# Attention and mixture layers on one core: no second score product in two of four head groups, an upper bound of the scores in its place, other slots in the last stage, first roots off GpSimd

## The reference

```python
q = _l2norm(q) * q_scale
k = _l2norm(k) * k_scale
sim = jnp.einsum('bhid,bhjd->bhij', q, k) * ATTN_SCALE
dist = -jnp.abs(cols[None, :] - (rows[:, None] + NUM_NULL_KV)).astype(sim.dtype)
sim = sim + dist[None, None] * slopes[None, :, None, None]
sim = jnp.where(causal_mask[None, None], neg, sim)
attn = jax.nn.softmax(sim, axis=-1)
out = jnp.einsum('bhij,bhjd->bhid', attn, v)
```

## Time and profile before

| | |
|---|---|
| three runs | 1751.26, 1755.71, 1756.75 us, median 1755.71 |
| the profiled execution | 1750.87 us, span 1749.1 us |
| mean granted clock of TensorE | 0.946 of 2.4 GHz |
| PE busy | 1565.2 us, 89% of the span |
| DVE, ACT, POOL busy | 1036.5, 774.6, 596.5 us |
| DMA | 73.77 MB, mean 42 GB/s |

### The profile page before, as it was taken

How to read it: one execution, slowest core, us unless ns; L and a number is a source line. 1 busy time by engine, 2 the same in 40 slices (tenths; PEclk the granted TensorE clock), 3 DMA queues, 4 the chain that set the end, 5 groups by cost and what they waited for, 6 DMA issues and landing times. The chain is left out here.

```text
span 1749.1 us, 28227 instructions
## 1 busy us (share of the span) xinstructions
PE 1565.2 (89%) x8941; PEld 740.7 (42%) x8941; DVE 1036.5 (59%) x2399; ACT 774.6 (44%) x1364; POOL 596.5 (34%) x597
## 2 busy tenths in 40 slices
PE   5799999999999999999999999999399549888898
PEld 2344444444444444444444444444267334333332
DVE  4455646666565655657656566665523277777775
ACT  3345454454544445544454444544144234444432
POOL 4253452534436354353543515442300331111000
PEclk8799999999999999999999999999599759999999
DMA  3502030320202202021120200000411100000000
GB/s 109 170 7 76 23 99 1 111 70 1 70 4 73 61 28 70 1 70 37 41 76 1 70 8 6 10 3 6 158 48 55 38 13 7 13 13 13 7 7 13
DMA packets 106718, 73.77 MB, mean 42 GB/s; under 512 B 5250, under 2 KB 100762, under 8 KB 106319
## 3 DMA queue, kind: packets, MB, share of 16 engines
q1 hardware_dynamic: 104526, 67.76, 12.7%
q0 software_dynamic: 2048, 4.20, 0.8%
HBM read 24.23 MB, written 47.71 MB: 41 GB/s over the span
## 5 line engine op out<-in xcount | busy, mean ns | idle before, releaser
L826 ACT ACTIVATE P<-S,keyb 128x386 f32<-128x386 f32 (+7 forms) x512 | 296.6, 630 | 375.8 <-PE S L609 375.6
L605 PE MATMUL S<-QT,KT 64*128 64x512 f32 (+5 forms) x1792 | 378.5, 478 | 8.3 <-DVE KT L964 6.3
L1200 POOL TENSOR_TENSOR rn<-nm,half 128x12 f32<-128x12 f32 x128 | 299.5, 2344 | 94.4 <-DVE nm L901 94.4
L1223 POOL TENSOR_SCALAR_AFFINE_SELECT P<-P 128x256 f32<-128x256 f32 (+1 forms) x256 | 156.3, 611 | 478.9 <-ACT P L826 478.7
L1004 DVE TENSOR_TENSOR Psum<-Psum,P 128x1796 f32<-128x1796 f32 (+7 forms) x256 | 281.9, 1101 | 37.5 <-PE O L630 18.3
L630 PE MATMUL O<-P,V 128*64 128x512 f32 (+5 forms) x1536 | 255.4, 436 | 4.0 <-POOL P L1223 3.3
L605 PEld LDWEIGHTS S<-QT,KT 64*128 64x128 f32 (+1 forms) x1792 | 158.4, 179 | 193.2 <-issue 183.6
L609 PE MATMUL S<-GQ,GK 64*128 64x512 bf16 (+5 forms) x896 | 150.9, 303 | 0.0
L466 PE MATMUL W<-xT,wts 128*128 128x512 f32 x256 | 141.3, 646 | 9.8 <-DVE QT L960 7.2
L1071 DVE TENSOR_TENSOR part<-W,rden 128x512 f32<-128x512 f32 x128 | 82.4, 686 | 83.4 <-PE W L678 83.4
L630 PEld LDWEIGHTS O<-P,V 128*64 128x64 f32 (+1 forms) x1536 | 80.0, 135 | 108.6 <-issue 94.2
(11 more groups left out here) (244 smaller groups left out, 2118.6 us busy)
## 6 DMA issues: line engine op xcount, KB each, us to landing
xg<-zero SPq DMA_DIRECT2D x16, 1216.0 KB, 10.6
yg<-zero SPq DMA_DIRECT2D x16, 1216.0 KB, 9.6
wts<-in_w_qkv SPq DMA_DIRECT2D x16, 384.0 KB, 3.8
gu<-in_gu SPq DMA_DIRECT2D x1, 2816.0 KB, 10.4
xb<-xg SPq DMA_DIRECT2D x40, 64.0 KB, 1.8
yg<-yb SPq DMA_DIRECT2D x40, 64.0 KB, 1.6
X<-in_x SPq DMA_DIRECT2D x4, 512.0 KB, 4.5
wo<-in_w_out SPq DMA_DIRECT2D x16, 128.0 KB, 2.3
```

What stands on the lines that cost most here:

```text
L605: nc.tensor.matmul(S[hh][0:m, at + c:at + c + w], KT[d, r, p, jt * P:jt * P + m], QT[d, r, p, Q0[jt] + c:Q0[jt] + c + w], start=True, stop ...
L826: nc.scalar.activation(probs(p, jt)[0:m, hh, 0:n], S[hh][0:m, at:at + n], ACT.Exp, bias=keyb[0:m, r, (2 * p + hh) * NKT + jt:(2 * p + hh) ...
L1200: nc.gpsimd.tensor_tensor(rn[:, c, u], nm[:, c, u], powers, ALU.pow).then_inc(rn_ok, 1)
L1223: nc.gpsimd.affine_select(own, own, [[0, 2], [1, w]], ALU.is_ge, 0.0, base=NNULL if jt == 0 else 0, channel_multiplier=-1).then_inc(cut, 1)
```

## The change

`FLAT` is the groups whose largest slope times 512 is below 40: groups 2 and 3, so the turns with n % 4 of 2 or 3, eight of 16 (the flat turns).

- In a flat turn `scores` issues no second product, and the first one ends the accumulation and signals ScalarE. Turns that prepare a flat one leave out both edge jobs: PE's transposes, ScalarE's copy to GQ, DVE's steps for E and `ee`, and 4 of the 12 root columns on GpSimd.
- In its place the keys' table of these groups is lifted by 40 and lowered by the largest score possible: the largest |q_scale x k_scale x 8|, found before attention by a matmul of ones with a diagonal (`lim`), a maximum over it, and one subtraction in `tabs`.
- The first turn's roots are made by ScalarE (square root) and DVE (a reciprocal and a Newton step, seven small operations a half) instead of GpSimd, `parts` stand in steps 5 and 10 instead of 9 and 12, the tables of laps are shorter, and ScalarE loads its tables at chosen places.
- In the last stage both choices, the weights and the weighings change slots; the share goes behind the down product; turned normed rows and router go one slot earlier; ScalarE takes the sigmoids' exponential ahead of the distances'. GpSimd gathers chunk 1 behind the first root instead of ahead of it.

```diff
+FLAT = tuple(g for g in range(NG) if slopes()[HG * g] * SEQ / 2 < LIFT)
...
+    for g in FLAT:
+        key[:, g * HG:g * HG + HG] += LIFT
...
-                return [k for k in AT if k[0] != "X" or n - 1 in HALF_AT]
+                return [k for k in AT if (k[0] != "X" or n - 1 in HALF_AT) and not (k in EDGE and flat_turn(n))]
...
-            AT_LAPS = {6: (2, 3), 9: (4, 5), 13: (6, 7)}
-            DVE_LAPS = {4: (2, 3), 9: (4, 5), 13: (6, 7)}
-            ACT_LAPS = {7: (2, 3), 10: (4, 5), 14: (6, 7)}
+            AT_LAPS = {6: (2, 3), 8: (4, 5), 9: (6, 7)}
+            DVE_LAPS = {4: (2, 3), 6: (4, 5), 8: (6, 7)}
+            ACT_LAPS = {7: (2, 3), 8: (4, 5), 10: (6, 7)}
...
-                            nc.tensor.matmul(S[hh][0:m, at + c:at + c + w], KT[d, r, p, jt * P:jt * P + m],
-                                             QT[d, r, p, Q0[jt] + c:Q0[jt] + c + w], start=True, stop=False)
-                        for hh in range(2):
+                            last = nc.tensor.matmul(S[hh][0:m, at + c:at + c + w], KT[d, r, p, jt * P:jt * P + m],
+                                                    QT[d, r, p, Q0[jt] + c:Q0[jt] + c + w], start=True, stop=flat_turn(t))
+                            if flat_turn(t) and c + w == n:
+                                last.then_inc(qk, 1)
+                        for hh in range(0 if flat_turn(t) else 2):
...
+                        pe.wait_ge(lim_ok, 3)
+                        nc.tensor.matmul(S[1][:, 512:512 + P], rows_n[:, 0:P], rows_n[:, P:2 * P], start=True, stop=True)
...
+                    nc.scalar.activation(flat[:, 0], nm[:, c].rearrange("p u n -> p (u n)"), ACT.Sqrt).then_inc(flat_ok, 1)
...
+                act.wait_ge(consts, 1)
+                nc.scalar.activation(warmed[:], half[:, 1, 0:1], ACT.Sqrt).then_inc(warm, 1)
...
+                act.wait_ge(warm, 1)
+                nc.scalar.activation(warmed[:], half[:, 1, 0:1], ACT.Exp).then_inc(warm, 1)
...
+                    nc.vector.tensor_scalar(b_, flat[:, 0], 1e-15, None, ALU.max).then_inc(step_ok, 1)
+                    nc.vector.reciprocal(y, b_).then_inc(step_ok, 1)
+                    nc.vector.tensor_tensor(a_, y, v, ALU.mult).then_inc(step_ok, 1)
+                    nc.vector.tensor_tensor(b_, a_, y, ALU.mult).then_inc(step_ok, 1)
+                    nc.vector.tensor_scalar(a_, b_, -0.5, 1.5, ALU.mult, ALU.add).then_inc(step_ok, 1)
+                    nc.vector.tensor_tensor(out, y, a_, ALU.mult).then_inc(step_ok, 1)
+                    nc.vector.tensor_tensor(rn[:, c, :, 2 * HG:], rn[:, c, :, 2 * HG:], nm[:, c, :, 2 * HG:],
+                                            ALU.mult).then_inc(step_ok, 1)
...
+                nc.vector.tensor_reduce(lim[:, 2:3], S[1][:, 512:512 + P], AX.X, ALU.max).then_inc(lim_ok, 1)
                 nc.vector.tensor_copy(w1q[:, 1, :], S[1][:, 0:D]).then_inc(m_ok, 1)
+                nc.vector.tensor_scalar(keys, keys, lim[:, 2:3], None, ALU.subtract).then_inc(lim_ok, 1)
...
-                    nc.gpsimd.tensor_tensor(rn[:, c, u], nm[:, c, u], powers, ALU.pow).then_inc(rn_ok, 1)
+                    w = (2 if flat_turn(n) else 3) * HG
+                    nc.gpsimd.tensor_tensor(rn[:, c, u, 0:w], nm[:, c, u, 0:w], powers[:, 0:w], ALU.pow).then_inc(rn_ok, 1)
...
-                    elif live(u - 2):
-                        share(u - 2, j)
                     if 0 <= k - LAG < KS:
                         down(k - LAG)
                     if j == 0 and live(u):
                         rows_turned(u)
-                    if j == 0 and live(u - 2):
-                        share(u - 2, 0)
+                    if live(u - 2):
+                        share(u - 2, j)
...
+                    if j == 3 and live(u - 1):
+                        logits(u - 1)
+                    if j == 3 and live(u + 1):
+                        arrive(u + 1)
                     if j == 4 and live(u - 1):
-                        logits(u - 1)
+                        pick_one(u - 1)
+                        pick_other(u - 1)
+                    if j == 5 and live(u - 1):
+                        weights(u - 1)
                     if j == 5 and live(u):
                         shares(u)
-                        weigh(u, 0)
-                    if j == 6 and live(u - 1):
-                        pick_one(u - 1)
-                    if j == 7 and live(u - 1):
-                        pick_other(u - 1)
+                    if j in (6, 7) and live(u):
+                        weigh(u, j - 6)
...
-                get_chunk(1)
                 periods(slot)
```

More of the change, by code:

```diff
@@ L241, in build @@
             scl = sb("scl", [P, 3], F32, sc)
+            lim = sb("lim", [P, 3], F32, sc)
             sums = sb("sums", [P, 2, 32], F32, sc)
@@ L277, in build @@
             xtr = sb("xtr", [P, CH], F32, sc)
+            flat = xtr[:, 0:4 * 4 * 3 * HG].rearrange("p (a n) -> p a n", a=4)
+            warmed = xtr[:, CH - 1:CH]
             rtop = sb("rtop", [P, 2, NB], F32, sc)
@@ L329, in build, with flat_turn, edged @@
             PREP_BEFORE = (("T1", "E0", ("R0", None), ("S00", "S01")), ("P00", "P02", ("P03", None), ("N0", None)))
+            def flat_turn(n):
+                return n % NG in FLAT
+            def edged(n, c):
+                return sum(0 if flat_turn(m) else 14 for m in range(n)) + (0 if flat_turn(n) else 7 * c + 7)
             def jobs(n):
-                return [k for k in AT if k[0] != "X" or n - 1 in HALF_AT]
+                return [k for k in AT if (k[0] != "X" or n - 1 in HALF_AT) and not (k in EDGE and flat_turn(n))]
             def prepared(n, k):
@@ L578, in prepare @@
                     for c in range(2):
-                        if AT[EDGE[c]] == at:
+                        if AT[EDGE[c]] == at and not flat_turn(n):
                             edges(n, c, alone)
@@ L804, in prepare @@
                                 square(n, c, j)
-                        if AT[EDGE[c]][:-1] == str(s):
+                        if AT[EDGE[c]][:-1] == str(s) and not flat_turn(n):
                             edges_out(n, r, c)
@@ L870, in _ @@
                             nc.scalar.copy(nkT[hh * DH:(hh + 1) * DH], src[hh * DH:(hh + 1) * DH, :, hh, :]).then_inc(null_te, 1)
+                    for c in range(2):
+                        if AT[TURNED[c]][:-1] == str(s):
+                            first_roots(c)
                     for h in ACT_LAPS.get(s, ()):
                         settled(h)
+                act.wait_ge(warm, 1)
+                nc.scalar.activation(warmed[:], half[:, 1, 0:1], ACT.Exp).then_inc(warm, 1)
                 turn(0, 0, True)
@@ L931, in parts @@
                         nc.vector.tensor_tensor(rres[:, k], own if k == 0 else rres[:, 0], R[:, at:at + 4, :, k], ALU.subtract).then_inc(r_ok, 1)
-                        dve.wait_ge(e_ok, ek + 2 * k + 2)
-                        hold(dve)
-                        nc.vector.tensor_copy(E[:, at:at + 4, :, :, k], heads(ee[:, k + 1])).then_inc(e_ok, 1)
+                        if edge:
+                            dve.wait_ge(e_ok, ek + 2 * k + 2)
+                            hold(dve)
+                            nc.vector.tensor_copy(E[:, at:at + 4, :, :, k], heads(ee[:, k + 1])).then_inc(e_ok, 1)
                         dve.wait_ge(r_ok, rk + 2 * k + 2)
@@ L1800, in slot @@
                         gate_up(u - 2, j)
[L1801 to L1807 removed]
+                    if j == 0 and live(u - 1):
+                        form(u - 1)
+                    if j == 0 and live(u - 2):
+                        combine(u - 2)
                     if 0 <= k - LAG < KS:
@@ L1817, in slot @@
                         last_turned(u - 3)
+                    if j == 2 and live(u - 1):
+                        normed_turned(u - 1)
                     if j == 3 and live(u - 1):
-                        normed_turned(u - 1)
-                    if j == 4 and live(u - 1):
                         route(u - 1)
@@ L2093, in slot @@
                         distances(u)
-                    if j == 4 and live(u + 1):
-                        arrive(u + 1)
-                    if j == 6 and live(u):
-                        weigh(u, 1)
-                    if j == 8 and live(u - 1):
-                        weights(u - 1)
                     if live(u - 2):
@@ L2139, in slot @@
                         norm1.pool_shift(pool, n4(u - 3))
-                    if j == 4 and live(u + 1):
+                    if j == 3 and live(u + 1):
                         norm.pool_shift(pool, n2(u + 1))
+                        if u < 0:
+                            get_chunk(1)
                         if live(u + 3):
```

90 lines of the change are left out of this document (63 added, 27 removed).

## The result

| kernel | median of 4 runs, us | range, us | ratio to before, 95% interval |
|---|---|---|---|
| before | 1753.49 | 1750.06 to 1756.75 | |
| changed | 1726.74 | 1724.99 to 1729.34 | 0.9849 [0.9823, 0.9875] |

The account below looks back on a forecast made before the run. PE was taken to bound attention (1127 of 1177 us busy). From the profiled 1750.9: attention -49, before it -3, six periods +1, filling +5.5 gave 1705.4, forecast 1708 with half the median's distance added; range 1687 to 1722.

Parts of the forecast that it names:

- The price of the second product: Attention, flat turns: start to start, 2.8 us a pair of heads, 5.6 a turn; 39 for seven turns, 3.5 for the last.
- What is late next: Attention, turn ends: PE's waits for roots and scales grow a little; 0.3 us a turn, 2 us in all, given back.
- The clock at the heads: Attention turn heads: clock fell behind 0.92 and 0.52 us waits at a quarter of heads; used for the last stage.
- a rival of many falls within flat turns: Attention: without the dense bf16 product the clock falls within flat turns; eight falls in each give 1808 us; chance 0.02.
- The edge transposes: Attention, eight preparations of flat turns: 16 groups of eight transposes at 0.55 us, 8.8 us saved on PE.
- Before attention: Ahead of the first score: roots on ScalarE and DVE instead of GpSimd give -3 us, between -7 and +2.
- the filling: Start of the last stage: choosing and weights now precede the weighings, so transposes come later; +5.5 us, between +2 and +8.
- The ring of the last stage: One period: transposes of sums, gate, silu, DVE's stretch to the second weighing and back; 38.3 us at full clock.
- The clock on it: Last stage: a fall in each period, 2.7 to 2.9 us, making periods 41.0 to 41.2; six periods +1.
- The chance of 0.20 for no falls: Rival: the clock stays up in the last stage, six periods at 38.3 save 16 us, 1692 with the addition; chance 0.20.
- attention gives back half: Rival: in flat turns GpSimd's cuts or the exponentials arrive after PE; +22 us, 1730 as a run; chance 0.10.

Follow-up runs that it names:

- the held runs: Second product, or edge transposes, put back into the changed kernel with later DVE additions and idle products (1707.79 us): 1735.60 and 1716.47 us.
- held_all: Changed kernel with later DVE additions and idle products in attention's waits, the last turn and the last stage: 1701.26 us, 0.9710 of before.
- before_filled: Kernel before, with 18 idle products ahead of share 7 in the last stage's six full periods: 1737.73 us, 0.9926 of before.
- slots_old: Changed kernel with the last stage's slots and first gathers put back as before: 1731.55 us, 0.9884 of before.

## Why the prediction was right or wrong

**The price of the second product: mis-sized.** "I take start to start" gave 2.8 us a pair, 5.6 a turn and 42.5 in all. The runs show at most 1.93 a pair, by the columns, 3.1 to 4.0 a turn at full clock, and 27.8 in all. The 0.22 for 512 columns was nearly right (at 2.4 GHz they are 0.213). The short ones were wrong: "386 and 258 columns as that" and 0.15 for the last two kinds, where 386, 258, 130 and 2 columns are 0.16, 0.11, 0.05 and nothing. The rest, down to 3.1, fits the places where PE waits for another engine once the product is gone (0.2 us for `rows_n` in the first pair, and the ends). That a start to start to another instruction holds something that stays when the product goes fits these numbers; no run shows what it is. The Trainium skill, "TensorE: Matmul & The Clock Gate", section "Back-to-back issue gap", gives columns / 2.4 + 2.5 ns for a single product. By it a turn would be 3.9 us, an estimate, and steps 9 and 10 agree with it (0.81 by the page, 0.80 and 0.81 in the traces); whole turns give less (3.1 to 4.0, 3.3 on average). This step is some 15 of the 34 us (42.5 forecast, 27.8 measured).

**What is late next: the step that failed.** The prediction read that DVE has "over 40% idle", gave back 2 us for grown waits, and held that "the removed 130- and 2-column pieces stood inside these waits". The 40% is an average over the stage. At the end of turn 2 DVE was busy for 9.7 of 10 us already before (270 to 280), and PE waited 0.92 behind it. Less work on PE then lengthens PE's wait: 0.92 to 1.73 for RT, and 0.6 to 1.93 for the router's choice. In all, PE's idle time in attention grew by 6.4 us where 2 were given back.

**The clock at the heads: taken for a rival's matter, priced too low.** Half-rate matmuls behind short waits stood in the earlier trace rows. I used them for the last stage, and in attention only as a rival of many falls within flat turns. It was one fall at the head of five or so turns, each of 2 to 4 us (0.88 for 0.38 in the earlier trace rows is one of its small ones). Between the prices of the held runs (27.8 + 8.7 = 36.5) and the 15.2 of attention 21.3 us are missing; less the 2 that were given back, these are the other 19 of the 34. Of these 6.4 are PE's longer idle time; the other 15 or so would be clock, an estimate that fits 47.7 us more at half clock. Filling the waits, which leaves DVE as late as it was and removes most of the falls, brought 11.1; with the additions moved as well 7.9 more; and the last turn's fill about 2.6 of the 6.5 of held_all: 21.6 in all. That this meets the 21.3 is not a proof: moved additions and filling might have helped the attention of the kernel before too, which had 13.7 us at half clock, and no run tries it. Nor were the product and the edges ever put back together.

**The edge transposes: right in size.** 8.8 forecast, 8.7 by the run, some 7 to 8 by the full-clock pieces.

**Before attention: right in size** (-3, measured -4.2; no run takes the new roots out, so the cause is not shown), **and the filling too** (+5.5, measured +6.2; second sums 29.9 behind the first instead of 22.8, and 5.9 back without the new slots).

**The ring of the last stage: right. The clock on it: wrong.** A period at full clock was worked out as 38.3; it is 38.2. The forecast took a fall in each period and 2.7 to 2.9 us for it. Four of the six were longer than 38.2: by 1.7 us twice, 1.2 and 0.7. The clock was below 1.00 in the sixth as well, without a cost. The chance of 0.20 for no falls and the forecast of all of them at full cost were both off; the truth lay between, and -10.3 is two thirds of the way to the rival's -16. The rule of the Trainium skill (same page, "HAM oscillation — how this bites in real kernels"), one long wait ahead of each tile, would have the clock stay up over the four short gaps; it did in one period of six (clock 1.00). The same page, "A second HAM failure mode: psum-queue depth-cycling", says that small idle times between groups of matmuls make the clock go up and down, at a cost between the bursts; the trace agrees: waits of 1.7 and 1.9 us stand ahead of the falls here, and with both filled (held_all) the falls are gone.

**What the new slots are worth.** In the measured kernel 10.3 less 6.2 for the filling, and 4.8 by the run without them. But before_filled shows that nearly all of the period's gain is the clock: 38.4 with the old slots once PE is kept busy, 38.2 with the new ones. By these figures the old slots with idle products would be the better choice, since the new ones give 0.2 a period, 1.2 in all, and cost 6 in the filling; that is an estimate, and no run has it.

**The rivals.** 1726.74 is the time of "attention gives back half", chance 0.10. Its place was right (a wait at the end of flat turns) but not its cause: neither cuts nor exponentials set it, but DVE's queue and the clock. So the meeting of the numbers is luck: the rival was also priced beside a last stage that came out better by 11.

## What to carry to other kernels

Cost a removed matmul by its columns at the granted clock and take off what PE will wait instead, and read the engine that hands over to PE in the very stretch where PE will arrive earlier, not its share of the whole. Where PE comes to wait for a microsecond or two between narrow matmuls, price a fall of the clock behind it and look at the matmuls that follow; a few idle products in the wait show in one run whether it is the clock. And an improvement that shows nothing by itself (the later additions, +2) can be worth some 6 us once the clock is held.

## What the runs showed of the hardware that was not expected

- Work that nobody reads made the kernel faster: six bf16 products of 128 x 512 (1.47 us) in a wait of 1.73 took the head behind it from 3.88 to 2.08 us; in all 11.1 us in attention, 13.7 in the kernel before (its last stage alone).
- Falls move. Putting the product back, or the edges, or shortening the waits did not remove them but put them at other turn heads (9.41 to 9.98, 8.6 to 9.8, 10.8 to 10.9 us). The same attention took 5.3 us less in another program (slots_old), with 44.4 us at half clock for 61.4. A gain below some 10 us on this kernel is a mixture of work and of where the falls lie.
- Waits of 1.7 and 1.9 us, the longest there, stood ahead of the stretches at half clock in the last stage. Nine idle products of 51 rows a period took away three of five such stretches, not the costly ones; with thirteen of 128 rows none began there, and the five periods behind the first are 38.20 to 38.25.
